# Output products of three head groups moved into the last attention group of the last batch; its last denominators taken straight from the exponents

## What is computed

```
Q = (x @ Wq.T).reshape(B, xN, 16, 32)                     # 16 heads of 32 columns
attn = softmax(einsum('bqhd,bkhd->bhqk', Q, K) * SCALE)   # over 750 context rows
O = einsum('bhqk,bkhd->bqhd', attn, V).reshape(B, xN, 512)
x = x + O @ Wo.T                                          # the output products
logits = einsum('bse,...') + gate_b                       # router: needs the new x
h = gelu(merged @ w1 + b1);  o = h @ w2 + b2              # 32 experts, w1 and w2 from HBM
```

## Time and profile before

| | |
|---|---|
| runs, us | 2315.62, 2317.16, 2319.82 |
| time of the profiled execution | 2323.09 us |
| its span, first to last instruction | 2321.4 us |
| TensorE busy | 1931.5 us (83%) |
| VectorE, ScalarE, GpSimd busy | 42%, 32%, 36% |
| DMA, mean over the span | 181 GB/s, 419.34 MB |
| mean granted clock of TensorE | 0.919 of full |

### The profile page before, as it was taken

One profiled execution on the slowest core, in us unless ns is written; L12 is line 12 of the kernel. 1 busy time (PEld: TensorE's weight loads), 2 busy tenths in 40 slices (PEclk: granted clock), 3 DMA queues, 4 the chain that ended last, 5 costly groups with the idle time before them and its releaser, 6 DMA issues. The chain is left out here.

```text
span 2321.4 us, 40341 instructions
## 1 busy us (share of the span) xinstructions
PE 1931.5 (83%) x12130; PEld 1138.9 (49%) x12130; DVE 974.4 (42%) x2473; ACT 748.8 (32%) x1551; POOL 827.3 (36%) x592
## 2 busy tenths in 40 slices
PE   7789999999999999999999999997665556655544
PEld 5466666666666666666666666653211111111111
DVE  1355655656656556565565665653100000000003
ACT  3243444435444344344443544432100000000000
POOL 0255554545555455555455555544000000000000
PEclk9999999999999999999999999997877777777777
DMA  6224223243242332423324223255699999999996
GB/s 179 71 68 105 61 75 90 74 102 71 68 98 76 87 86 68 97 70 78 89 74 104 66 71 95 76 169 203 247 419 422 420 420 421 421 421 421 421 377 244
DMA packets 139167, 419.34 MB, mean 181 GB/s; under 512 B 32780, under 2 KB 74988, under 8 KB 114556
## 3 DMA queue, kind: packets, MB, share of 16 engines
q1 hardware_dynamic: 131484, 409.73, 51.8%
q10 hardware_dynamic: 6656, 8.15, 1.0%
q0 software_dynamic: 992, 1.02, 0.1%
HBM read 306.39 MB, written 16.15 MB: 139 GB/s over the span
## 5 line engine op out<-in xcount | busy, mean ns | idle before, releaser
L1072 DVE TENSOR_REDUCE maxes<-bank 112x1 f32<-112x376 f32 (+1 forms) x1024 | 506.7, 538 | 204.7 <-PE bank L1272 203.9
L886 ACT ACTIVATE probs<-bank 125x448 f32<-125x448 f32 x768 | 402.7, 547 | 369.0 <-PE bank L1294 362.4
L1294 PE MATMUL bank<-q_st,k_st 98*125 98x224 f32 x1536 | 384.0, 339 | 21.5 <-DMA q_st<-max_lo 10.3
L764 POOL TENSOR_TENSOR psum_keys<-psum_keys,probs 125x896 f32<-125x896 f32 x128 | 269.1, 2102 | 327.8 <-ACT probs L886 322.2
L1656 PE MATMUL bank<-ring,hid_T 128*32 128x512 f32 x1024 | 177.9, 857 | 199.7 <-DMA ring<-in_L_ffn_w 196.4
L1272 PE MATMUL bank<-k_st,q_st 96*112 96x376 f32 (+1 forms) x1024 | 324.0, 367 | 13.2 <-DVE maxes L1072 7.6
L1294 PEld LDWEIGHTS bank<-q_st,k_st 98*125 98x125 f32 x1536 | 265.2, 192 | 132.2 <-issue 68.8
L767 POOL TENSOR_TENSOR psum_keys<-psum_keys,probs 125x896 f32<-125x896 f32 x128 | 267.7, 2092 | 10.0
L1574 DVE TENSOR_TENSOR o_fin<-bank,b_row 16x512 f32<-16x512 f32 x32 | 21.7, 679 | 589.3 <-PE bank L1614 589.3
L1497 POOL DMA_DIRECT2D o_rows<-o_fin x31 | 15.3, 493 | 598.1 <-DVE o_fin L1574 598.1
L1629 PE MATMUL bank<-ring,tok 128*32 128x512 f32 x1024 | 145.2, 693 | 76.4 <-DMA ring<-in_L_ffn_w 74.3
(11 more groups left out here) (149 smaller groups left out, 2268.6 us busy)
## 6 DMA issues: line engine op xcount, KB each, us to landing
ring<-in_L_ffn_w SPq DMA_DIRECT2D x128, 2048.0 KB, 30.5
k_st<-k_hi SPq DMA_DIRECT2D x512, 93.8 KB, 2.2
k_st<-k_lo SPq DMA_DIRECT2D x256, 93.8 KB, 2.2
q_st<-q_hi SPq DMA_DIRECT2D x504, 28.0 KB, 1.8
ctx_nat<-in_ctx SPq DMA_DIRECT2D x16, 750.0 KB
x_in<-in_x SPq DMA_DIRECT2D x16, 448.0 KB, 3.6
out<-x SPq DMA_DIRECT2D x16, 448.0 KB, 8.1
out<-ring ACTq DMA_DIRECT2D x28, 256.0 KB, 3.1
```

The lines of the kernel that those rows point to most:

```text
L764: nc.gpsimd.tensor_tensor(psum_keys[:], psum_keys[:], lo, ALU.add).then_inc(pool_chain, 1)
L886: nc.scalar.activation(probs[n % 2][:, j, :], bank[5 + u % 2][0:SK, 0:2 * T], ACT.Exp, scale=SCALE).then_inc(probs_ready, 1)
L1072: nc.vector.tensor_reduce(maxes[:, j, t, c:c + 1], bank[2 + n % 3][0:TT, 0:SC[c + 1] - SC[c]], AX.X, ALU.max).then_inc(s_drained, 1)
L1294: last = nc.tensor.matmul(bank[5 + u % 2][0:SK, kk * T:(kk + 1) * T], k_st[slot][:, j, k * SK:(k + 1) * SK], q_st[slot][:, j, :], start=Tr ...
```

## The change

In the last batch only, four edits:

1. TensorE makes six of the eight output products early. `begin_out("out0")` stands at step 7 of group 3 (behind unit 6) and `begin_out("out1")` at step 11 (behind unit 10). Each makes the three products of groups 0 to 2.
2. In the tail, `out0` and `out1` make only the product of group 3, on top of what stands in their banks, and no longer wait for those banks.
3. GpSimd no longer adds the last third of group 3 to `psum_keys` (two operations fewer).
4. The last denominators are made by `last_denominators`: 12 products instead of 4. Four read `psum_keys` (first two thirds), and eight read the exponents of the last third directly.

```diff
+BEGIN_OUT = {(3, 7): "out0", (3, 11): "out1"}
...
-                            if s in SUM_AT:
+                            if s in SUM_AT and not (kind == "last" and (kt, SUM_AT[s]) == (3, 2)):
                                 sum_keys(b, kt, SUM_AT[s])
...
-                    if prev:
+                    if prev and not (kind == "tail" and job[:3] == "out"):
                         wait_out(pe, *prev)
...
                         pe.wait_ge(o_ready, bb * 4 + 4)
-                        for kt in range(G):
+                        for kt in (G - 1,) if kind == "tail" else range(G):
                             last = nc.tensor.matmul(ps[0:TT, :], tokens(o_T[:, kt, :], i),
                                                     wo_T[:, kt, :], start=(kt == 0),
                                                     stop=(kt == G - 1))
...
+                def last_denominators():
+
+                    p = probs[(3 * G - 1) % 2]
+                    pe.wait_ge(keys_summed, B * 12 - 1)
+                    for n in range(3):
+                        for j in range(4):
+                            part = p[:, j, (n - 1) * T:n * T] if n else psum_keys[:, j, :]
+                            last = nc.tensor.matmul(bank[7][j * HD:(j + 1) * HD, T:2 * T],
+                                                    ones[0:SK, 0:HD], part,
+                                                    start=(n == 0), stop=(n == 2))
+                    last.then_inc(den_done, 1)
+
+                def begin_out(job):
+
+                    wait_out(pe, *before(job, "tail", LAST + 1))
+                    pe.wait_ge(o_ready, LAST * 4 + (G - 1))
+                    for kt in range(G - 1):
+                        nc.tensor.matmul(bank_of(job, "tail")[0:TT, :],
+                                         tokens(o_T[:, kt, :], OUT[job][2]), wo_T[:, kt, :],
+                                         start=(kt == 0), stop=False)
...
                         if kind == "tail":
                             values(b - 1, G - 1, 2)
-                            denominators(b - 1, G - 1)
+                            last_denominators()
...
+                            if kind == "last" and (kt, s) in BEGIN_OUT:
+                                begin_out(BEGIN_OUT[kt, s])
                             if s in PV_AT:
                                 values(b, kt, PV_AT[s])
```

## The result

| | before | after |
|---|---|---|
| median of 20 runs each, us | 2318.95 | 2312.68 |
| lowest and highest, us | 2315.04, 2325.22 | 2307.71, 2316.66 |
| ratio after to before, 95% interval | | 0.9973, 0.9965 to 0.9980 |
| span of the profiled execution, us | 2321.4 | 2306.9 |
| mean granted clock | 0.919 | 0.920 |

The changed kernel is 6.3 us faster by the medians (4.6 to 8.1 by the interval). 2312.5 was forecast, from a median that twenty runs put 1.8 us higher; of the gain itself 4.7 us were forecast.

The account below looks back on a forecast made before the run. TensorE was taken to bound the first stage, the weight stream the second, which can only begin earlier. 7.1 - 2.3 - 2.8 + 0.4 - 7.1 = -4.7 us, from 2317.16 to 2312.5 us; range 2309.5 to 2317.0.

Parts of the forecast that it names:

- What bounds: Whole kernel: TensorE bounds the first stage, the weight stream the second, which can only begin earlier, not be shortened.
- Inserted: Last group: the moved output products add 4.5 us for `out0` and 2.6 us for `out1`, +7.1 us.
- Rest of the group: Units 7 to 11 and two thirds of `values`: 5.0 us at 2.4 GHz instead of 7.3, -2.3 us.
- GpSimd's wait and denominators: Behind the values: TensorE's wait for GpSimd's additions goes, -2.8 us; 24 denominator passes instead of 8 cost +0.4 us.
- Normalise: From the end of the denominators to the first output pass: keeps its length, 1.75 us.
- Tail products: Output passes left in the tail: four in 1.9 us instead of 16 in 8.96 us, -7.1 us.
- Cover: Last group: early products' waits cost nothing, and GpSimd's sum of the second third is ready 2 us before the denominators.
- The store: SyncE's store of x behind slot 7's load: 0 us lost, at worst 1 us; it lands 3.1 us after issue.
- the rival: Store of x queues behind slot 7's load on SyncE: +1 us, gain -3.7 us, 2313.5 us; chance 10%.
- Clock late: Last group: the clock rises only in the second moved stretch; gain -1.3 us, 2315.9 us; chance 9%.
- clock low throughout: Clock stays at 1.2 GHz to the end of the output products: +3.4 us, 2320.6 us; chance 6%.
- Faster gate product: Tail: the gate product also speeds up, up to 1.5 us more; -6.2 us, 2311.0 us; chance 12%.

Follow-up runs that it names:

- dens_only: The changed kernel with all 16 output passes back in the tail, so only the last denominators differ from the kernel before; timed -4.5 us to the kernel before, ratio 0.9987.
- dummy_run: The kernel before plus six output passes that nobody reads behind unit 7 of the last group; timed +1.8 us, ratio 1.0012.
- pause_filled: The changed kernel plus eight passes that nobody reads in TensorE's pause ahead of the last group; timed -12.2 us to the kernel before, ratio 0.9946.
- in_pause: The changed kernel with four of the six moved products made in the pause ahead of the last group; timed -13.2 us to the kernel before, ratio 0.9947.
- pause_warm: in_pause plus passes that nobody reads in three later pauses, up to the first expert; timed -16.9 us to the kernel before, ratio 0.9929.
- outs_only: The changed kernel with the last denominators and GpSimd's additions as before, so only the output products move; timed -0.4 us to the kernel before, ratio 1.0004.
- warm: The changed kernel plus ten idle passes in the tail, between last output product and router's transposes; timed -8.1 us to the kernel before, ratio 0.9963.
- pieces: The changed kernel with the six moved products one at a time behind units 5 to 10; timed -7.3 us to the kernel before, ratio 0.9969.

## Why the prediction was right

The sign and the mechanism came out as forecast; the gain was 4.7 us by the sum and 6.3 us measured. That the time agrees to 0.2 us is luck: the gain was 1.6 us larger than the sum, and the median from which it was subtracted 1.8 us lower than that of twenty runs. Step by step, in the profile after:

- *What bounds.* Held: in every kernel of the study group to x plus x to load tells the timed difference to within 2.4 us (by these and timed: dens_only -3.5 and -4.5 us, dummy_run +3.6 and +1.8, pause_filled -9.9 and -12.2, in_pause -12.3 and -13.2, pause_warm -16.5 and -16.9). The second stage only starts earlier.
- *Inserted.* 7.1 us predicted, 3.4 + 2.2 = 5.6 measured from the start of each run to the start of the next unit. This is the term that was off. I took the 3.9 us that the clock had needed from the start of the tail products; here the rise came 2.7 us in at the latest. That old run followed 1.75 us without passes, the moved one follows a busy group, which may be the reason. The same run of six passes took 3.4 to 4.0 us in six profiles (3.38, 3.43, 3.54, 3.62, 3.69, 3.96), so the point of the rise scatters. The second run costs 2.2 and not 2.6 us, since I counted the last pass up to its end and the next unit starts before.
- *Rest of the group.* 5.0 us predicted. From 1595.23 to the end of the values, 1606.35, are 11.1 us; less 5.6 that is 5.5. The wait for ScalarE behind unit 7 is 0.50 us where I counted 0.3; the rest is the end of the last pass that the term above gave up.
- *GpSimd's wait and denominators.* -2.4 us predicted. From the end of the values to the end of the denominators: 1607.84 to 1611.59 is 3.75 us before, 1606.35 to 1607.49 is 1.14 after: -2.6.
- *Normalise.* 1.65 us instead of 1.75. *Tail products.* 1.98 us, 1.9 predicted.
- Sum with the measured terms: 5.6 - 1.8 - 2.6 - 0.1 - 7.0 = -5.9 us, as group to x has it. The profile's other 0.6 us (6.5 with them) lie in x to load, where the first expert's passes took 5.17 us instead of 6.04.
- *Cover.* The early products' waits cost nothing: the first run begins 6.99 us into the group, where unit 7 stood before (7.00). GpSimd's sum of the second third, forecast to be ready 2 us ahead of the denominators, ends at 1604.39 us, 1.8 ahead of them.
- *The store.* It lands 3.1 us after its issue as before, and ScalarE starts 3.16 us behind the second addition in both kernels. The meeting that the rival needs took place: slot 7 was issued at 1604.71 and landed 7.8 us later, at 1612.5, 0.6 us behind the issue of the store. The store was no later for it, so the rival falls in this profile.
- *Clock late, clock low throughout.* Neither in the two profiles of the change. *Faster gate product*: no, 3.17 us.

One argument of the prediction was weaker than it looked: it treated the edits as a sum of terms that could be had one by one. outs_only shows that the clock hangs on the wait for GpSimd. Had only the products been moved, the same way of adding would have forecast 3 us where nothing came.

What stays open: whether executions without a profile have the clock low in the last group as often as these (every profile without a filled pause shows it). The gains of the timed runs fit the profiles' to within 2.4 us, which speaks for it, but doesn't show it. Why the point of the rise lies between 2.4 and 3.5 us behind the start of the first run of six passes in the six profiles, and why the clock fell ahead of the tail products in in_pause and not in pause_warm, stays open too. Nor was it tried why the clock fell behind the transposes in warm.

## What to carry to other kernels

Where an engine's clock follows its work, read a wait twice: its own length, and what the passes behind it cost at the low clock; a removed wait can be worth more than its length, and a moved product less. Before moving work, look for the pause that costs the clock: filling it, even with passes that nobody reads, can be worth as much as the move itself (3.7 us against 3.5 here, by group to x). Price a piece that is one of two with the other undone, for the halves need not add up.

## What the runs showed of the hardware

- The granted clock fell from 1.00 to 0.50 in a pause of 3.3 to 3.7 us without passes, or within 0.3 us behind it (outs_only, pieces), in each of the nine profiles whose pause ahead of the group was left empty, and did not in the three where passes filled it.
- It also fell around shorter ones: 0.7 us into a pause that followed waits of 0.50 and 0.93 us (dummy_run), and in the 1.65 us for `normalise` in in_pause, but not in the same 1.65 us in pause_warm.
- With TensorE busy 14.67 of 15.80 us, mostly with score passes and passes of 32 columns, the clock stayed at 0.50 (dens_only); where two passes of 512 columns stood among them, it was up some 3 us later (pieces). In dens_only it rose without wide passes, behind values and 24 denominator passes in one piece.
- Idle products cost no time in a pause of 3.65 us in which TensorE waits for a DMA, and the kernel was 4.9 us faster by the medians with them (pause_filled).
